# Softplus shared otherwise between ScalarE and VectorE, in a fused kernel whose order a planner writes

## What is computed

```
delta = jax.nn.softplus(dt + b_dt)          # layer 0: 256 channels; layer 1: 512 channels
h     = exp(delta * A) * h + (delta * u) * B # the scan: one step a token, for each of 32 (16) states
y     = sum over states of h * C
```

## Time and profile before

| | us |
|---|---|
| median of 3 runs | 1470.28 (1461.58 to 1472.63) |
| the profiled execution | 1470.09 |
| its span in the trace | 1468.8 |
| PE / DVE / ACT / POOL busy in the span | 1175.3 / 1001.7 / 626.0 / 572.0 |
| mean granted clock of TensorE | 0.922 |

### The profile page before, as it was taken

How to read it: one execution, slowest core, us unless ns; L and a number is a source line. 1 busy time by engine, 2 the same in 40 slices (tenths; PEclk the granted TensorE clock), 3 DMA queues, 4 the chain that set the end, 5 groups by cost and what they waited for, 6 DMA issues and landing times. The chain is left out here.

```text
span 1468.8 us, 18356 instructions
## 1 busy us (share of the span) xinstructions
PE 1175.3 (80%) x5952; PEld 919.8 (63%) x5952; DVE 1001.7 (68%) x1807; ACT 626.0 (43%) x1667; POOL 572.0 (39%) x471
## 2 busy tenths in 40 slices
PE   4557346696786898799979888899979879999787
PEld 2335223565675686587758676777857658777665
DVE  6887899889997998899984579943343233333333
ACT  5344555456673344587642154634421024343100
POOL 2565466764686674588750038810000000000000
PEclk9788679899797999799989989999989999999899
DMA  4651134432563552276532136533312332221232
GB/s 136 245 183 59 46 116 136 129 111 87 142 188 132 158 181 90 77 219 194 183 130 73 47 129 218 181 103 97 126 65 86 108 125 98 97 98 55 86 108 72
DMA packets 91808, 180.30 MB, mean 123 GB/s; under 512 B 9296, under 2 KB 28688, under 8 KB 91456
## 3 DMA queue, kind: packets, MB, share of 16 engines
q1 hardware_dynamic: 78016, 166.15, 35.8%
q10 hardware_dynamic: 13696, 12.98, 2.7%
HBM read 165.07 MB, written 14.02 MB: 122 GB/s over the span
## 5 line engine op out<-in xcount | busy, mean ns | idle before, releaser
L1921 DVE TENSOR_TENSOR_SCAN scan_banks<-scan_banks,h_end,drive 128x256 f32<-128x256 f32 x512 | 359.8, 744 | 11.3 <-ACT scan_banks L1650 6.3
L2281 POOL TENSOR_TENSOR sum<-sum,state 128x512 f32<-128x512 f32 x174 | 222.2, 1277 | 121.3 <-DVE state L1931 120.8
L2260 POOL TENSOR_TENSOR drive<-w0T,bc_rows 128x512 f32<-128x512 f32 x128 | 164.3, 1285 | 108.7 <-DVE scan_banks L1921 46.3
L2260 POOL TENSOR_TENSOR drive<-w1T,bc_rows 128x512 f32<-128x512 f32 x128 | 162.8, 1273 | 101.5 <-DMA bc_rows<-bc_rows 34.8
L2284 POOL TENSOR_TENSOR stats_b<-stats_b,neg_half 128x2 f32<-128x2 f32 x12 | 8.4, 702 | 497.4 <-DVE stats_b L2091 294.0
L1931 DVE TENSOR_TENSOR state<-scan_banks,bc_rows 128x512 f32<-128x512 f32 x256 | 174.0, 680 | 0.1
L2106 DVE TENSOR_REDUCE soft<-score_banks 128x1 f32<-128x128 f32 (+7 forms) x128 | 95.8, 754 | 114.4 <-PE score_banks L1505 113.5
L1503 PE MATMUL score_banks<-kv,qT 128*128 128x512 f32 (+3 forms) x384 | 149.3, 504 | 18.9 <-ACT probs L1812 16.5
L1353 PE MATMUL score_banks<-state,ident 128*128 128x256 f32 x256 | 84.6, 467 | 81.9 <-DVE state L1931 81.7
L1812 ACT ACTIVATE probs<-score_banks,soft 128x128 f32<-128x128 f32 (+7 forms) x128 | 94.6, 740 | 91.0 <-DVE soft L2106 89.2
L1650 ACT ACTIVATE scan_banks<-delta1T,a 128x256 f32<-128x256 f32 x256 | 111.9, 473 | 37.9 <-DVE state L1931 29.1
(11 more groups left out here) (217 smaller groups left out, 2139.2 us busy)
## 6 DMA issues: line engine op xcount, KB each, us to landing
bc_rows<-bc_rows SPq DMA_DIRECT2D x256, 256.0 KB, 3.5
streamed_w<-in_w_head SPq DMA_DIRECT2D x64, 384.0 KB, 5.0
expert_w<-in_w_moe SPq DMA_DIRECT2D x52, 384.0 KB, 4.1
kv_past<-kv ACTq DMA_DIRECT2D x48, 256.0 KB, 4.0
kv<-in_w_moe SPq DMA_DIRECT2D x32, 384.0 KB, 3.7
kv<-kv_past SPq DMA_DIRECT2D x16, 768.0 KB, 4.7
kv<-kv_past SPq DMA_DIRECT2D x16, 512.0 KB, 4.8
streamed_w<-in_w_moe SPq DMA_DIRECT2D x16, 384.0 KB, 3.2
```

The costliest lines, as they stand in the source:

```text
L1921: done = e.engine.tensor_tensor_scan(states, states, drive[g % len(drive)][:, i, 0:size], h_end[layer][:, n, kt:kt + 1], ALU.mult, ALU.add)
L2260: self.tt(drive[g % len(drive)][:, :, 0:size], w_of(layer, c)[:, PAIR * half:PAIR * (half + 1), 0:size], rows_of(g, c, 0), ALU.mult).then_ ...
L2281: self.tt(to, so_far, slot_of(c, layer, k), ALU.add).then_inc(added, 1)
```

## The change

Three things. ACT also makes max(x,0) (Relu, two operations of 256 columns from PSUM, right behind |x|) and `above` = 1 + exp(-|x|) (one copy of 512 columns between the exponential and the logarithm). DVE drops L1960 and L1970 and works in four operations: e' = (above - 1) - e, l' = min(above - 1, l), x' = x - e', `delta` = x' + l'; the product `w` stays. DVE no longer has a stage before the logarithm. The planner is told of the new stages, and its estimate of a PE operation of n columns goes from 0.018 + 0.00175 n to 0.025 + 0.0019 n, which is 0.466 to 0.511 us at 256 columns. New semaphores are left out of the diff.

```diff
@@ -192,7 +192,7 @@
 
 
 def pe(*columns):
-    return "pe", sum(0.018 + 0.00175 * n for n in columns)
+    return "pe", sum(0.025 + 0.0019 * n for n in columns)
 
 
 def pe_turn(n):
@@ -398,16 +398,14 @@
 
     def softplus(self, c, g, given, use):
         p, size, layer = self.p, SIZES[c], min(g, 1)
-        yield Stage(partial(p.softplus_abs, c, g), (act(size, size),), (given,), (("abs", c, g),),
+        yield Stage(partial(p.softplus_in, c, g), (act(*[size] * 4),), (given,), (("in", c, g), ("read", *use)),
                     user=("softplus", c, g))
-        yield Stage(partial(p.softplus_x, c, g), (dve(size, size),), (("abs", c, g),),
-                    (("x", c, g), ("read", *use)))
-        yield Stage(partial(p.softplus_log, c, g), (("act", 2 * TABLE + act(2 * size, 2 * size)[1]),),
-                    (("abs", c, g),), (("log", c, g),))
+        yield Stage(partial(p.softplus_log, c, g), (("act", 2 * TABLE + act(*[2 * size] * 3)[1]),),
+                    (("in", c, g),), (("log", c, g),))
         b = c - 1 if layer else c - 2
         before = (("decays", b, layer), ("drives", b, layer)) if b >= 0 else ()
-        yield Stage(partial(p.softplus_sum, c, g), (dve(size, *[2 * size] * 5),),
-                    (("log", c, g), ("x", c, g), *before), (("delta", c, g), ("scratch", "softplus", c, g)))
+        yield Stage(partial(p.softplus_sum, c, g), (dve(*[2 * size] * 5),),
+                    (("log", c, g), *before), (("delta", c, g), ("scratch", "softplus", c, g)))
 
     def first(self):
         p = self.p
@@ -1673,7 +1672,8 @@
                     self.dma(bc_of(0, c)[:, k, :], dbc[RANK0 + k * STATE0:RANK0 + (k + 1) * STATE0, 0:size]
                              ).then_inc(rows_stored[0].sem, 16)
 
-            def softplus_abs(self, c, g):
+            def softplus_in(self, c, g):
+
                 e, size, layer, half = self.e, SIZES[c], min(g, 1), max(g - 1, 0)
                 name = "b_dt1" if layer else "b_dt0"
                 b = bank_of("delta", c, half) if layer else bank_of("dt", c)
@@ -1685,13 +1685,19 @@
                 for k in range(2):
                     self.activation(hid[:, 2 + k, 0:size], b[:, k * size:(k + 1) * size], ACT.Abs,
                                     bias=col(name, 2 * half + k)).then_inc(sp_abs[layer].sem, 1)
+                for k in range(2):
+                    self.activation(hid[:, k, 0:size], b[:, k * size:(k + 1) * size], ACT.Relu,
+                                    bias=col(name, 2 * half + k)).then_inc(sp_x[layer].sem, 1)
 
             def softplus_log(self, c, g):
+
                 e, size, layer, half = self.e, SIZES[c], min(g, 1), max(g - 1, 0)
                 es, ls = hid[:, 2:4, 0:size], hid[:, 4:6, 0:size]
+                above = by_tile(s[:, 0:KD * size], size)
                 e.wait_ge(sp_abs[layer], c, 2 * half + 1)
                 self.activation(es, es, ACT.Exp, scale=-1.0).then_inc(sp_exp[layer].sem, 1)
                 e.wait_ge(sp_exp[layer], c, half)
+                self.activation(above, es, ACT.Copy, bias=1.0).then_inc(sp_above[layer].sem, 1)
                 self.activation(ls, es, ACT.Ln, bias=1.0).then_inc(sp_ln[layer].sem, 1)
 
             def to_channels(self, c, j):
@@ -1950,36 +1956,25 @@
 
 
 
-            def softplus_x(self, c, g):
-                e, size, layer, half = self.e, SIZES[c], min(g, 1), max(g - 1, 0)
-                name = "b_dt1" if layer else "b_dt0"
-                b = bank_of("delta", c, half) if layer else bank_of("dt", c)
-                wait_scratch(e, "softplus", c, g)
-                e.wait_ge(sp_abs[layer], c, 2 * half + 1)
-                for k in range(2):
-                    self.ts(hid[:, k, 0:size], b[:, k * size:(k + 1) * size], col(name, 2 * half + k), 0.0, ALU.add,
-                            ALU.max).then_inc(sp_x[layer].sem, 1)
-
             def softplus_sum(self, c, g):
+
+
                 e, size, layer, half = self.e, SIZES[c], min(g, 1), max(g - 1, 0)
                 xs, es, ls = (hid[:, 2 * i:2 * i + 2, 0:size] for i in range(3))
-                cs = by_tile(s[:, 0:KD * size], size)
+                above = by_tile(s[:, 0:KD * size], size)
                 to, to_w = (t(layer, c)[:, 2 * half:2 * half + 2, 0:size] for t in (delta_of, w_of))
-                e.wait_ge(sp_exp[layer], c, half)
-                self.settle()
-                self.ts(cs, es, 1.0, -1.0, ALU.add, ALU.add).then_inc(*self.order.tick())
+                e.wait_ge(sp_above[layer], c, half)
                 e.wait_ge(sp_ln[layer], c, half)
-                self.settle()
-                self.tt(ls, ls, cs, ALU.min).then_inc(*self.order.tick())
-                self.settle()
-                self.tt(cs, es, cs, ALU.subtract).then_inc(*self.order.tick())
                 e.wait_ge(sp_x[layer], c, 2 * half + 1)
                 self.settle()
-                self.tt(cs, cs, xs, ALU.add).then_inc(*self.order.tick())
+                self.stt(es, above, 1.0, es, ALU.subtract, ALU.subtract).then_inc(*self.order.tick())
+                self.stt(ls, above, 1.0, ls, ALU.subtract, ALU.min).then_inc(*self.order.tick())
+                self.settle()
+                self.tt(xs, xs, es, ALU.subtract).then_inc(*self.order.tick())
                 self.settle()
                 wait_unit(e, decayed, c - 1 if layer else c - 2, layer)
                 wait_unit(e, driven, c - 1 if layer else c - 2, layer)
-                self.tt(to, cs, ls, ALU.add).then_inc(delta_ready[layer].sem, 1)
+                self.tt(to, xs, ls, ALU.add).then_inc(delta_ready[layer].sem, 1)
                 e.wait_ge(delta_ready[layer], c, half)
                 if layer:
                     e.wait_ge(hs_ready, c)
```

More of the change, by code:

```diff
@@ L157, in nothing @@
         pass
-    load = load_x = dbc = project_dt = softplus_abs = softplus_x = softplus_log = softplus_sum = chore = nothing
+    load = load_x = dbc = project_dt = softplus_in = softplus_log = softplus_sum = chore = nothing
     fetch = decay = drive = scan = weigh = carry = add_up = skip0 = skip1 = nothing
@@ L984, in build_program @@
         sp_ln = [signal("softplus0_ln", 1), signal("softplus1_ln", 2)]
+        sp_above = [signal("softplus0_above", 1), signal("softplus1_above", 2)]
         sp_x = [signal("softplus0_x", 2), signal("softplus1_x", 4)]
```

## The result

The change makes the kernel slower. Its median is 1492.99 us (1486.85 to 1495.56) against 1465.93 (1459.88 to 1472.63) for the kernel before, measured beside it; the ratio is 1.0189, 95% interval 1.0158 to 1.0219. The prediction said 1469, range 1444 to 1488, most likely no change: wrong, on the slow side, by 24 us.

What follows compares the result with a forecast made beforehand. VectorE was taken to set the pace to 779.1 us, a chain mixed with TensorE work to 866.0, VectorE to 968.2, then TensorE; 729 + 60 + 108 + 571 and 1.3 gave 1469 us, no change, range 1444 to 1488.

Steps and rivals of the forecast that it cites:

- A to B: From the end of chunk 3's `skip0` (A) to its second layer 1 softplus `w` (B): 86.9 us before, 60 forecast.
- the softplus' saving on VectorE: Shorter softplus on VectorE: 1.87 us a call, 22.4 us for 12 calls, 18.7 for the ten ahead of 779.1.
- To A: Start to the end of chunk 3's `skip0`: 779.1 us less 42 of VectorE load and 8 of credit, 729.
- I take half: Softplus on VectorE: half of the 981 ns of delays a call assumed to stay; bounds 2357 or 1376 ns saved.
- rival 3: Softplus saving smaller, through GpSimd contention and ScalarE's 1.57 us in three exposed calls: 11 us more, 1480; chance 0.10.
- The credit of 8 us for waits on TensorE: Up to 770 us: a third of VectorE's 26.7 us of waits for TensorE vanishes; bounds 0 and 23.
- B to C: From the second layer 1 softplus to chunk 3's `project_y`, the last scans: VectorE load 100 at 0.93 busy, 108 us.
- Behind C: After chunk 3's `project_y`, attention and experts: 500.6 us plus 70 for 65 us more TensorE load, 571.
- the tail's own rate: After chunk 3's `project_y`: 432 us of TensorE load in 500.6 us, which prices the added 65 at 75.
- Rival 1: Faster: TensorE work put off behind the last scans costs nothing; 1450 or 1448 us; chance 0.34.
- Rival 2: Slower: last chunk's chain stays at 87 us and the 8 us credit fails; 1504, half of both 1487; chance 0.20.
- 27 + 8 + 11: Upward bounds: A to B not shrinking, the wait credit failing, a smaller softplus saving; about half reach 1488.

Runs made afterwards that it cites:

- new_ops_old_order: The new softplus operations with the planner told the old stages, costs and estimate, so all streams keep the order of the kernel before: 1462.33 us, ratio 0.9976.
- above_in_psum_old: As new_ops_old_order, but `above` is written over the call's own PSUM bank instead of SBUF, so the bank is released later: 1479.87 us, ratio 1.0105.

## Why the prediction was wrong, step by step

Two terms of the sum failed. The larger is the stretch from A to B, put at 60 us, under both ways of working it out, where 71.1 were measured. The other is the softplus' saving on VectorE, put at 1.87 us a call where it was 1.20.

**To A: 729 foreseen, 736.3 measured.** The term that failed is the softplus' saving, taken as 1.87 us a call: it was 1.20, which is 6.7 us over the ten calls and nearly all of the 7.3. "I take half" of the delays was the choice; all stayed and some came on top. The bounds were also built wrongly: they let the old operations' delays stay or go, but what stays depends on which GpSimd operations happen to run beside: 257 ns a call in the order of before, 1152 in this one. The row in time, GpSimd's and VectorE's:

```profile
148.31 1.64 POOL L2276 TENSOR_TENSOR sum<-sum,state 128x512 f32<-128x512 f32 x1 [5.51 <-DVE state L1937]
```

```profile
148.15 0.68 DVE L1970 SCALAR_TENSOR_TENSOR hiddenT<-sT,hiddenT 128x512 f32<-128x512 f32 x1
148.75 1.75 DVE L1971 SCALAR_TENSOR_TENSOR hiddenT<-sT,hiddenT 128x512 f32<-128x512 f32 x1
150.54 0.69 DVE L1973 TENSOR_TENSOR hiddenT<-hiddenT 128x512 f32<-128x512 f32 x1
```

L1971 took 1.75 us in the eight calls in which a GpSimd operation ran beside it and 0.68 to 0.69 in the other four. So rival 3 was right on VectorE's operations in this order, and the saving fell below the bound on which it rested. The credit of 8 us for waits on TensorE did come in: ten groups and 26.7 us became nine and 17.4 up to 725 us, 9.3 less. The two that answer to those rows:

```profile
DVE soft L2101 <- PE score_banks L1504: 3.1, 5, 1.5
...
DVE stats L1990 <- PE work_bank L1336: 0.8, 5, 0.2
```

Against it, all waits for ScalarE together grew from 33.8 to 39.3 us in the same stretches; those at the scans and at the softplus alone grew by 9.4:

```profile
DVE scan_banks L1927 <- ACT scan_banks L1649: 12.8, 7, 4.2
DVE hiddenT L1970 <- ACT hiddenT L1701: 12.4, 3, 10.5
```

where before, up to 770 us, it was

```profile
DVE hiddenT L1960 <- ACT hiddenT L1686: 8.2, 6, 6.6
...
DVE scan_banks L1921 <- ACT scan_banks L1650: 6.3, 5, 2.7
...
DVE hiddenT L1973 <- ACT hiddenT L1695: 1.3, 1, 1.3
```

25.2 us against 15.8. In net the credit held: up to A VectorE's idle time fell from 87.4 to 78.4 us, 9.0 less. Its busy time fell by 33.8 us (691.7 to 657.9), where the prediction's count of work had 42 less. So the miss to A lies in the work and not in the waits. (The prediction's 44 us of TensorE work put off up to A is 45 by its own table; nothing hangs on it.)

**A to B: 60 foreseen, 71.1 measured; the largest miss.** The evidence was read rightly: the six feed-forward stages took 8.9 us (745.34 to 754.28), as chunk 0's 9.4 promised, in place of 18.6. But of two estimates, 64 by the old rate and at most 78 by the old length less that saving, I took neither: 60, below both. Their mean is what came. VectorE was idle for 37 of the 71.1 us, in a chain of latencies that TensorE's load doesn't measure. On VectorE, the wait for the feed-forward's last product and the one ahead of the first layer 1 softplus:

```profile
761.33 0.88 DVE L2036 SCALAR_TENSOR_TENSOR sT<-work_bank,cols,xT 128x256 f32<-128x256 f32 x2 [5.53 <-PE work_bank L1330]
...
794.14 0.69 DVE L1970 SCALAR_TENSOR_TENSOR hiddenT<-sT,hiddenT 128x512 f32<-128x512 f32 x1 [11.20 <-ACT hiddenT L1701]
```

and on ScalarE what ends the second:

```profile
789.36 0.84 ACT L1686 ACTIVATE hiddenT<-work_bank,cols 128x256 f32<-128x256 f32 x2 [0.24 <-PE work_bank L1330]
...
792.13 1.28 ACT L1701 ACT_TABLE_LOAD   x1
793.42 0.63 ACT L1701 ACTIVATE hiddenT<-hiddenT 128x512 f32<-128x512 f32 x1
```

From |x| to VectorE's first operation behind the logarithm it is 4.78 us (789.36 to 794.14); before it was 3.47, from these two rows:

```profile
849.77 0.84 ACT L1686 ACTIVATE hiddenT<-work_bank,cols 128x256 f32<-128x256 f32 x2 [1.96 <-PE work_bank L1331]
```

```profile
853.24 0.69 DVE L1973 TENSOR_TENSOR hiddenT<-hiddenT,sT 128x512 f32<-128x512 f32 x1 [0.65 <-ACT hiddenT L1695]
```

So the first of the last chunk's two calls comes 1.3 us later there. The second took 7.00 us from |x| (796.98 to 803.98), before 6.06 (856.27 to 862.33), 0.9 more. I had left both in the range. The remaining excess of some 9 us over the 60 is not taken apart by any run.

**B to C: 108 foreseen, 107.0 measured.** Right: VectorE's load at its pace.

**Behind C: 571 foreseen, 574.9 measured.** The mechanism was right, 65 us of load put off; I took 70, between the full rate and the tail's own rate of 75, and 74.3 was the price. The tail's own rate was the right term.

**The rivals.** Rival 1, that the put-off work costs nothing, had 0.34 and is refuted by the tails of the table of orders, which grow with every step of load: its own argument against it, that the tail's order and rate don't change, decided. Rival 2 came in part: A to B shrank by less than foreseen, but to 71.1, under the 76 that I named as the point where it decides, and the credit, its other half, did not fail; the slower side was reached without that, because three misses of one sign added up. The range let two of them come together downward and stopped short of half way upward: half of 27 + 8 + 11 is 23 and would have given 1492, still under the median.

**The error behind the sizes.** I set a gain of 71 us up to C against a loss of 70 behind it, from terms with different certainty. The loss was well priced, by one rate over a long stretch with one engine 88% busy. Of the gain every term leaned on a favourable choice: half of the delays, a credit for waits, a stretch shorter than both ways of working it out. Of the three only the credit came in. The sum was close to zero only by these choices; with a cautious value of each (1.38 us a call, no credit, 71 as the mean of 64 and 78, and the tail's own rate) it would have been about 1469 + 5 + 8 + 11 + 4 = 1497. That this is near the measured 1493 is in part luck, as it leaves out a credit that came in and allows 5 us for delays that cost 6.7.

**What would have shown it.** A at 725 to 740 came true, a tail of 565 to 575 too, `project_y` at 897 didn't (914.5), nor A to B of 55 to 65. VectorE's waits for TensorE did not grow; its waits for ScalarE did.

## To carry to other kernels

When an edit moves work from a stretch bound by one engine to a stretch bound by another, price both ends: here the work cost on average 1.19 us a microsecond of TensorE load where it went, and gave 0.47 where it left, where VectorE set the pace. Fewer busy microseconds on the bounding engine are worth what is left after its new waits: 23.5 us of VectorE work taken away in an unchanged order gave 3 to 7, since VectorE then waited longer for ScalarE's logarithm. A delay beside another engine is a matter of the order as much as of the operation: the softplus' second operation was held up in 8 of 12 calls in one order and in 1 of 12 in the other. And look at what an operation releases as well as at what it makes: two activations put 3 us later held a PSUM bank, and that cost more than the latency they had been in the way of.

## What the runs showed of the hardware

- A VectorE operation with two SBUF inputs, right behind another such and with a GpSimd operation running beside it, took 1.75 us in place of 0.68, in 8 of 8 such calls of the change and 1 of 1 in `new_ops_old_order`; GpSimd's operation took 1.64 to 1.72 us in place of 1.27. With one of the inputs in PSUM (`above_in_psum_old`) the same two VectorE operations took 0.67 to 0.69 us in all 12 calls, with GpSimd beside them or not. The delayed end, 150.50, is GpSimd's end, 149.95, and 0.55 us, and it was 0.54 to 0.56 us in all nine: the VectorE operation gets going about when GpSimd's is over. The Trainium skill's page "SBUF — State Buffer", section "Who interferes with whom", says that the port pair which the two engines share is an exclusive lock, and these rows agree.
- ScalarE's copy of 512 columns took 602 ns into PSUM (`above_in_psum_old`) and 630 into SBUF (the change).
- In the first 125.8 us behind C, with TensorE 90% busy, the granted clock was 1.00, its upper level of 2.4 GHz throughout (0.97 in the 449.6 us after), against 0.91 to 0.92 in the stretches ahead of it (78% to 85% busy), part of which ran at 1.2 GHz. Put-off work met the higher clock there, and cost its length all the same.
